# Self-attention: the inverse of the softmax sums as a power on GpSimd, and P normalised by a diagonal while it is turned

## What is computed

```python
q, k, v = heads(h @ wq), heads(h @ wk), heads(h @ wv)      # 16 heads of width 16 (first layer) or 64 (the others)
scores = einsum('bhld,bhsd->bhls', q, k) * scale           # 512 x 512 for each head and batch row
probs = softmax(scores, axis=-1)
x = x + merge(einsum('bhls,bhsd->bhld', probs, v)) @ wo
```

## Time and profile before

| what | value |
| --- | --- |
| median of three runs | 5093.72 us (5093.52 to 5094.57) |
| the profiled execution's own time | 5091.53 us |
| its span, first to last instruction | 5089.6 us |
| TensorE busy | 4705.9 us, 92% |
| VectorE busy | 3726.7 us, 73% |
| GpSimd busy | 2708.1 us, 53% |
| ScalarE busy | 2257.5 us, 44% |
| first, second, third self-attention | 2326 to 2798, 3092 to 3674, 4102 to 4683 us |

### The profile page before, as it was taken

How to read it: one execution, slowest core, us unless ns; L and a number is a source line. 1 busy time by engine, 2 the same in 40 slices (tenths; PEclk the granted TensorE clock), 3 DMA queues, 4 the chain that set the end, 5 groups by cost and what they waited for, 6 DMA issues and landing times.

```text
span 5089.6 us, 53152 instructions
## 1 busy us (share of the span) xinstructions
PE 4705.9 (92%) x18768; PEld 2603.1 (51%) x18768; DVE 3726.7 (73%) x3613; ACT 2257.5 (44%) x3966; POOL 2708.1 (53%) x1431
## 2 busy tenths in 40 slices
PE   7888899898988888878999899999999999999999
PEld 4555555555555555434555544555554445555544
DVE  4999999999999999886777625666654256665531
ACT  5556555555556555534444434334333233334331
POOL 2666666666666666556888215666521056665210
PEclk9999999999999999998999999999999999999999
DMA  3444444444444444430000100000101000001000
GB/s 117 152 155 153 158 142 158 152 155 156 154 153 158 153 156 151 144 111 7 1 1 13 40 19 1 1 1 1 46 5 42 0 1 1 1 1 50 1 1 17
DMA packets 110962, 372.64 MB, mean 73 GB/s; under 512 B 28016, under 2 KB 32880, under 8 KB 107760
## 3 DMA queue, kind: packets, MB, share of 16 engines
q1 hardware_dynamic: 110704, 369.26, 20.6%
HBM read 365.94 MB, written 3.28 MB: 73 GB/s over the span
## 4 chain that ended last, share of the span: by engine, by line
PE 49%; DVE 3%; ACT 1%; POOL 1%; issue 1%; DVEq 0%; ACTq 0%; POOLq 0%
PE PS L1160 7%; PE PS L1170 6%; PE PS L1185 6%; PE PS L1139 5%; PE PS L1349 5%; PE PS L1360 3%; PE PS L1148 3%; PE PS L1196 2%; PE PS L1309 2%; PE PS L1270 2%; PE PS L1279 1%; PE PS L1296 1%; PE PS L1288 1%; PE PS L1126 1%; ACT PA L1434 1%
## 5 line engine op out<-in xcount | busy, mean ns | idle before, releaser
L635 POOL TENSOR_TENSOR UH<-UH,BC 128x1152 f32<-128x1152 f32 x512 | 1344.2, 2625 | 920.0 <-DVE U L683 920.0
L1101 POOL TENSOR_SCALAR PA<-PA,INV 128x512 f32<-128x512 f32 x768 | 1189.6, 1569 | 551.6 <-DVE INV L1621 551.6
L691 DVE TENSOR_TENSOR_SCAN UH<-DA,U 128x1152 f32<-128x1152 f32 x512 | 1307.2, 2553 | 24.4 <-ACT DA L575 7.0
L384 PE MATMUL Y<-UH,ident_sb 128*128 128x512 f32 (+1 forms) x3072 | 1117.5, 508 | 201.7 <-DVE ZS L698 104.8
L384 PEld LDWEIGHTS Y<-UH,ident_sb 128*128 128x128 f32 x3072 | 568.0, 196 | 788.4 <-issue 539.4
L1434 ACT ACTIVATE PA<-PS,NMX 128x512 f32<-128x512 f32 x768 | 519.4, 684 | 720.5 <-DVE NMX L1615 566.3
L575 ACT ACTIVATE DA<-DT,NEGA 128x575 f32<-128x575 f32 x1024 | 718.9, 763 | 101.3 <-DVE UH L691 67.3
L683 DVE TENSOR_TENSOR U<-DTX,BC 128x1152 f32<-128x1152 f32 x512 | 698.9, 1365 | 56.5 <-DMA BC<-bc_rows 10.1
L1630 DVE COPY VP<-PS 128x512 f32<-128x512 f32 x768 | 495.2, 686 | 256.9 <-PE PS L1170 235.2
L1615 DVE TENSOR_REDUCE NMX<-PS 128x2 f32<-128x1024 f32 x384 | 452.5, 1219 | 58.4 <-PE PS L1160 58.4
L1170 PEld LDWEIGHTS PS<-ident_sb,PA 128*128 128x128 f32 x3072 | 351.8, 142 | 241.4 <-issue 193.5
(11 more groups left out here) (153 smaller groups left out, 4929.6 us busy)
## 6 DMA issues: line engine op xcount, KB each, us to landing
BC<-bc_rows SPq DMA_DIRECT2D x512, 576.0 KB, 3.7
ARENA<-mamba_a SPq DMA_DIRECT2D x16, 1421.0 KB, 7.4
ARENA<-pair_w SPq DMA_DIRECT2D x4, 3072.0 KB, 10.3
WB<-mamba_b SPq DMA_DIRECT2D x16, 514.0 KB, 5.0
VP<-ff_w SPq DMA_DIRECT2D x2, 3072.0 KB
WO<-out_w SPq DMA_DIRECT2D x4, 1024.0 KB
stream<-x_t SPq DMA_DIRECT2D x2, 1024.0 KB, 9.9
ARENA<-pair_w SPq DMA_DIRECT2D x4, 512.0 KB, 5.5
```

Source lines behind the costliest of these rows:

```text
L384: mm = pe.matmul(Y[:, a:b], IDENT[:, :], UH[:, SLOT[j], a:b], start=(s == 0), stop=(s == DS - 1), skip_group_check=True)
L635: pool.tensor_tensor(h, h, BC[:, j % NBB, 1, :].unsqueeze(1).broadcast_to([P, HK, T]), ALU.mult).then_inc(s_hc, 1)
L691: dve.tensor_tensor_scan(UH[:, SLOT[j], :], DA[:, j % NDA, :], U[:, 0:HC], 0.0, ALU.mult, ALU.add).then_inc(s_scan, 1)
L1101: pool.tensor_scalar(PR[:, n % 3, j, :], PR[:, n % 3, j, :], INV[:, n % 4, j:j + 1], None, ALU.mult).then_inc(s_ps, 1)
```

## The change

Two buffers are added, MINUS (128 x 2, set to -1 once by POOL) and DIAG (128 x 3 x 2 x 128, three steps deep). DVE's inverse(n) is gone in all places. POOL waits for the exponentials of step n itself (s_p), makes INV = SUM to the power of MINUS on 128 x 2, waits for its own result (s_r) and for turn(n-3) (s_tp), and then multiplies the identity, 128 x 128, by each head's inverse into DIAG: a diagonal matrix of the inverses. P stays as ACT wrote it. The turn is no longer pe.transpose(PR tile, identity) but pe.matmul with the PR tile as stationary and DIAG as moving operand: (P tile) transposed, times the diagonal, which is the turned and normalised tile. The counts of s_r, s_ps and s_tp stay as they were.

```diff
--- before.py
+++ after.py
@@ -909,6 +909,8 @@
         NMX = sb("NMX", [P, 4, 2])
         SUM = sb("SUM", [P, 4, 2])
         INV = sb("INV", [P, 4, 2])
+        MINUS = sb("MINUS", [P, 2])
+        DIAG = sb("DIAG", [P, 3, 2, P])
         CST = sb("CST", [P, 2, 3, 8])
         LSQ = sb("LSQ", [P, 2, KD, S0])
         LRS = sb("LRS", [P, 2, S0])
@@ -965,7 +967,7 @@
         s_mx = step("t_max")
         s_p = step("t_exps")
         s_r = step("t_inverse")
-        s_ps = step("t_probs_scaled")
+        s_ps = step("t_inverse_diagonals")
         s_tp = step("t_probs_turned")
         s_pt = step("t_probs_t_ready")
         s_pv = step("t_pv")
@@ -1071,6 +1073,8 @@
             @block.gpsimd
             def _(pool):
                 pool.memset(EPSC[:, :], EPS).then_inc(s_zero, 1)
+                pool.memset(MINUS[:, :], -1.0).then_inc(s_zero, 1)
+                pool.wait_ge(s_zero, START + 2)
 
                 def zero_blocks():
                     pool.memset(KB[:, :, :, :], 0.0).then_inc(s_kbz, 1)
@@ -1096,9 +1100,12 @@
                 for l in range(NT):
                     for n in range(NN):
                         ng = l * NN + n
+                        pool.wait_ge(s_p, START + 2 * ng + 2)
+                        pool.tensor_tensor(INV[:, n % 4, :], SUM[:, n % 4, :], MINUS[:, :], ALU.pow).then_inc(s_r, 1)
                         pool.wait_ge(s_r, START + ng + 1)
+                        pool.wait_ge(s_tp, START + 2 * (ng - 2) if ng >= 3 else START)
                         for j in range(2):
-                            pool.tensor_scalar(PR[:, n % 3, j, :], PR[:, n % 3, j, :], INV[:, n % 4, j:j + 1], None,
+                            pool.tensor_scalar(DIAG[:, ng % 3, j, :], IDENT[:, :], INV[:, n % 4, j:j + 1], None,
                                                ALU.mult).then_inc(s_ps, 1)
                     for at in range(NITS + 5):
                         if at in CN_AT[l]:
@@ -1167,8 +1174,8 @@
                             pe.wait_ge(s_ps, START + 2 * ng + j + 1)
                             pe.wait_ge(s_pt, START + 2 * ng + j - 1 if ng else START)
                             for kt in range(QT):
-                                mm = pe.transpose(PS[:, B_T + j, kt * P:(kt + 1) * P], PR[:, n % 3, j, kt * P:(kt + 1) * P],
-                                                  IDENT[:, :])
+                                mm = pe.matmul(PS[:, B_T + j, kt * P:(kt + 1) * P], PR[:, n % 3, j, kt * P:(kt + 1) * P],
+                                               DIAG[:, ng % 3, j, :], start=True, stop=True)
                             mm.then_inc(s_tp, 1)
 
                     def values(it, half):
@@ -1615,11 +1622,6 @@
                         dve.tensor_reduce(NMX[:, n % 4, :], PS[:, B_S + 2 * (n % 2):B_S + 2 * (n % 2) + 2, :], AX.X, ALU.max,
                                           negate=True).then_inc(s_mx, 1)
 
-                    def inverse(n):
-                        ng = l * NN + n
-                        dve.wait_ge(s_p, START + 2 * ng + 2)
-                        dve.reciprocal(INV[:, n % 4, :], SUM[:, n % 4, :]).then_inc(s_r, 1)
-
                     def copies(n):
                         ng = l * NN + n
                         hh, i = n // 2, n % 2
@@ -1647,8 +1649,6 @@
                     query(0)
                     shift(0)
                     shift(1)
-                    inverse(0)
-                    inverse(1)
                     for it in range(NITS):
                         tt = it // PPT[l]
                         last = it % PPT[l] == PPT[l] - 1
@@ -1657,7 +1657,6 @@
                             if n + 2 < NN:
                                 shift(n + 2)
                                 shift(n + 3)
-                                inverse(n + 2)
                             if i == 0 and last and tt + 1 < ALLT[l]:
                                 query(tt + 1)
                             if i == 2 and it >= NP and 1 <= it % NP <= KD:
@@ -1667,8 +1666,6 @@
                                 dve.wait_ge(s_cent, START + LN_AT[l][it] + 1)
                                 dve.sem_inc(s_pjf, 1)
                             copies(n)
-                            if n + 3 < NN:
-                                inverse(n + 3)
                             if i == 0 and it and (it - 1) % PPT[l] == PPT[l] - 1:
                                 output((it - 1) // PPT[l])
                             copies(n + 1)
```

## The result

The changed kernel takes 5404.74 us, median of four runs (5402.32 to 5406.61), beside 5094.15 us for the kernel before on the same chip: a ratio of 1.0609, 95% interval 1.0591 to 1.0628. The forecast was 5430 us in a range of 5374 to 5513.

A forecast was written before the change was run, and what follows sets the result against it. TensorE was taken to bound the three self-attentions. The turn as a product, +356 us, and idle and clock regained, -20 us, gave +336 us on the kernel before: 5430 us, range 5374 to 5513.

The forecast's parts named there:

- the growth of the gap: TensorE's gap at a turn's waits grows with the longer weight load: +41 us at most, a third taken, +14.
- what comes back: First self-attention: 12 us of TensorE's idle and 8 us of clock loss return, -20 us.
- Two records in place of one: TensorE's turn: each of 3072 calls leaves two records as a product, not one as a transpose, 6144 in all.
- Their price: Turn on TensorE: 0.111 us a record from the cross-attention chain, 0.89 us a step, +342 us.
- the first rival: Turn on TensorE: a product costs its busy share, 134.8 ns a record, +414 us, 5498 us; chance 12%.
- The reason given for the gap: Turn on TensorE: its 0.22 us gap stands before and after, since both turns wait on the same two semaphores.
- GpSimd at nothing: Self-attentions: power 0.5 us and diagonals 0.46 each, a 1.4 us step, hidden under TensorE; even a 3.14 us power hidden.
- The line through a one-column memset: Diagonal's price on GpSimd, from shortest and present instruction: 2.88 ns a column, 0.46 us for 128 x 128.
- VectorE's reciprocals at nothing: Self-attentions: removing 384 reciprocals, 63.6 us of VectorE busy time, gains nothing itself, as TensorE bounds the last two layers.
- POOL as the bound: Self-attentions: a slow power makes GpSimd the limit; at 6 us a power, about 6080 us; chance 4%.
- Four times the transpose: Turn on TensorE: a product takes four times a transpose, +1014 us, 6088 us; chance 1%.
- The faster side: Turn costs nothing more, its second record hidden or absent, so only idle and clock are gained: 5067 us; chance 2%.

The follow-up runs named there:

- experiment 2: The changed kernel with the turn again the transpose with the identity, diagonals made but unused, P not normalised: 5059.54 us, ratio 0.9928.
- experiment 7: The changed kernel with TensorE waiting once ahead of both heads of a turn, not ahead of each: 5408.25 us, ratio 1.0616.
- experiment 9: The changed kernel with the transpose turn and VectorE's reciprocal back, GpSimd making only unused diagonals, P not normalised: 5084.98 us, ratio 0.9981.
- experiments 3 and 4: The changed kernel with GpSimd's power made twice, and six times, into spare buffers: 5405.78 us, ratio 1.0610, and 5558.32 us, ratio 1.0909.
- experiment 6: The changed kernel with the inverse made by VectorE's reciprocal again, GpSimd making only the two diagonals: 5403.27 us, ratio 1.0606.
- experiment 1: The kernel before with the turn as an ordinary product with the identity, GpSimd's multiplication and VectorE's reciprocal kept: 5407.17 us, ratio 1.0611.
- experiment 4: The changed kernel with GpSimd's power made six times, the extra ones into spare buffers: 5558.32 us, ratio 1.0909.
- experiment 5: The kernel before with the inverse made by GpSimd as a power, its multiplications and the transpose kept, VectorE's reciprocal gone: 5146.2 us, ratio 1.0099.
- experiments 8 and 10: The kernel before with the second head's P multiplied by ScalarE: 5094.97 us; the same with the inverse as GpSimd's power, not VectorE's reciprocal: 5075.17 us.

## Why the prediction was right

The forecast was too high by 25 us, and both mis-sized terms erred to the same side: 11 us are the growth of the gap (+14, where the turn's busy time grew by 2.8 more than the 342), 11 what comes back (-20, where it was -31.4), and 2 that the median run no longer lies above the profiled one. Its steps held in this way:

- **Two records in place of one** held exactly: 6144 records. **Their price** was put at 0.111 us from the chain in cross-attention, +342 us; the turn grew by 344.8 us of busy time, and kernels that differ in the product alone (experiment 2 against the changed kernel) lie 345 us apart. The busy mean of 134.8 ns, the first rival, would have been +414.
- **The growth of the gap**, +14 us, was the first mis-sized term: the mean turn was 1.09 - 0.87 = 0.22 us over its records before and is 1.99 - 1.78 = 0.21 after. The longer weight load does not lengthen it. The reason given for the gap, the two semaphores ahead of a turn, is not borne out: with one pair of waits taken away it stayed (experiment 7).
- **What comes back**, -20 us, was the second: it is 313.4 - 344.8 = -31.4 us. The idle of the first self-attention went from 21.9 to 3.5 us where I had 12 back. Of the clock I took 8 back from three stretches; by the whole stage, 0.96 of 472 us is 38 us at the lower level and 19 lost, 0.99 of 554 is 11 and 5.5, so some 13 came back. Outside the self-attentions the span grew by 3.7 us, most of it in the stretch between the first two, which differs by as much among executions with the same instructions there (experiment 9). The first stage was put at 571 us and took 552, the others at 701 and 700 and took 700.7 and 702.7.
- **GpSimd at nothing** held, though both its prices were too low: the power 0.72 us for 0.5, the diagonal 0.61 for 0.46, a step of 1.93 for 1.4 us. The cover of several microseconds carried it, and experiments 3 and 4 show between which steps it ends. That even a power of 3.14 us would be hidden was too bold: with diagonals of 1.21 us POOL's step would be 4.35 us beside PE's 4.31 (an estimate from both groups). The line through a one-column memset was a poor way to a price: from 128 to 512 columns POOL's tensor_scalar takes (1569 - 606) / 384 = 2.5 ns a column on top of 0.29 us.
- **VectorE's reciprocals at nothing** held for this kernel (experiment 6), but the reason covered less than it seemed. I wrote that the first stage would get its idle back by the distance that a longer turn gives; it does (experiment 1). That the reciprocal in VectorE's queue had a part in that idle I had not seen: 25 of 35 us by the medians in the order of experiments 9 and 2, 9.9 of 23.1 by the first self-attention alone. In the changed kernel it does not show (experiment 6).
- **The rivals.** POOL as the bound: out by a factor of four in the power's price, with its mechanism shown (experiment 4). Four times the transpose: out, as it is twice. The faster side needed a second record under 9 ns.
- **On the clock**, the rule of the Trainium skill (TensorE: Matmul & The Clock Gate, Part 4) that transpose mode does not count as busy in the same way did not show its effect here: experiment 2 holds 1.00 with transposes from 2400 us on, and experiment 5, with transposes, has a stage at 0.97 where experiment 4, with products, has 0.96. That stretches fell because PE idled in them, as I took it, is not borne out either: experiment 5 idled 56 us in this stage and its clock was no lower than that of the kernel before with 21.9. What lets the clock fall stays open.

## What to carry to other kernels

A turn that also scales looks free since both are one call, but in f32 a transpose leaves one record and a product two; look in the profile for a line that already does the product in this shape, and take its price from the chain, not from its busy mean. Work taken off an engine that is not the bound gains only what the bound engine idles and what its clock loses (35 us in experiment 2), so anything added to the bound engine must cost less than that. And look for short instructions that make a queue wait for another engine: taking a reciprocal of 166 ns off VectorE gave 20 us by the medians between experiments 8 and 10 and 25 between 9 and 2, while half of GpSimd's multiplication, moved to ScalarE, gave none.

## What the runs showed of the hardware that was not expected

- A power on 128 x 2 elements on GpSimd takes 719 ns, more than a multiplication of 128 x 128 (606 ns), and 0.66 us in the chain when it follows another.
- An f32 product of 128 x 128 x 128 costs the same by a diagonal and by the identity, 124 ns of busy time a record in the turn, and these and the product by data in cross-attention all take 0.111 us a record in an unbroken chain.
- A turn is 0.2 us longer behind scores or values than behind a projection (1.98 against 1.78 us); as transposes the turns were at 1.02 and 1.20 against 0.87. A change of the waits within it moved nothing; its cause is open.
